# Returning expert results to their tokens' rows inside the routed loop instead of gathering them at the end

## The chip, the cores and the metric

The kernel runs on one core of a Trainium2 chip. The metric is the device time of one execution in microseconds (us), the median of several runs. The profile is one execution, whose span runs from its first to its last instruction.

## The reference

A cross-attention block is followed by a mixture-of-experts feed-forward part. Only the second part is touched in substance. There are 4 x 1024 = 4096 tokens of 256 channels, all in fp32:

```
x = x + cross_attention(context, layernorm(x), mask)
f = layernorm(x)                                      # "tokens"
shared = gelu(f @ Wfc_s + bfc_s) @ Wproj_s + bproj_s  # 256 -> 1024 -> 256
p = softmax(f @ Wr); the two largest of 8, divided by their sum, are the gates
routed = sum over the two chosen experts e of gate_e * (gelu(f @ Wfc[e] + bfc[e]) @ Wproj[e] + bproj[e])
out = x + shared + routed
```

## The kernel before

It is six blocks, one after another: `prepare` (layer norms, weights cut into high and low parts), `attention` (about two thirds of the time; it also clears the DRAM tensor `routed` with one DMA of the ACT queue), `project_out` (writes `tokens`), `route` (computes `slots`, the row in `routed` of each of the 2 x 4096 token-expert pairs), `experts` and `combine`.

**experts.** Rows are worked on in tiles of 256: m = 0 to 15 are the shared expert's (SHARED = 16), m = 16 to 55 the routed experts' (ROUTED = 40). In step m, TensorE (PE) alternates between the first layer of tile m+1 (`fc`, four parts) and the second layer of tile m (`proj`, four parts), and after `proj` part 2 transposes the input of tile m+2. That is 100 matrix instructions a step. ACT does the gelu and the high half of the second weights (`upper_w2`), DVE cuts the hidden values (`hidden`), cuts the transposed input (`lower_x`) and adds the bias into `y[:, s]` (s is m's parity), and POOL makes the low half of the second weights (`lower_w2`, line 1342, twice a step). Each matrix product is three matmuls of high and low parts.

The SP queue issues, in a fixed order per routed step m: the load of the input `xt` of tile m+2 (`load_x`), four quarter loads of the first weights of tile m+3, two half loads of the second weights of tile m+2, the small first bias, then, behind a wait for `y` of tile m (`s_yv`), the store of `y` to `ys` (line 1315) and the load of the second bias. So the next step's `load_x` is queued behind that wait.

During the shared tiles POOL fills `routed`: for each of 32 tiles of 128 tokens it loads the tile into one of four buffers `moved` (line 1355) and, three tiles later, writes each row of it to its two places in `routed` with two indirect DMAs (line 1361). Before it loads into a buffer again it waits for both scatters from it. SP's first `load_x` from `routed` (step 14, for tile 16) waits until all 64 scatters have landed (line 1289).

**combine.** For 16 pairs of 128-token tiles POOL gathers rows of `ys` with four indirect DMAs a pair (line 1545), into four buffers `c_y`. DVE multiplies them by the gates and adds them to `x2` (line 1559, four instructions a pair), and SP stores the pair to the output (line 1566).

Of the kernel before, what the change touches and what calls it, by code (L numbers as in the profile page):

```python
# [5 lines left out]
F32 = mybir.dt.float32  # L6
# [29 lines left out]
ROUTED += ROUTED % 2  # L36
ROWS = (ROUTED + 1) * TS


# [314 lines left out]
def attention(nc, qn_g, kn_g, lnT, wHead, maskRow, maskCol, attT, routed, Wfc_s, Wfc, w1S):  # L354
# [6 lines left out]
    with ExitStack() as ctx:  # L361
# [28 lines left out]
        o_sb = t.sb("o_sb", [DH + 1, 2, 512])  # L390
        zero = t.sb("zero", [P, D])
        gain2 = t.sb("gain2", [P, DH])
        most2 = t.sb("most2", [P, 1])
# [32 lines left out]
        def _(sp):  # L426
# [56 lines left out]
            either(sp, attend)  # L483
            sp.wait_ge(s_clear, 16)
            for q in range(QB):
# [6 lines left out]
        def _(pool):  # L492
# [156 lines left out]
        def _(act):  # L649
            def window(w):  # L650
                for u in range(UNITS):
# [11 lines left out]
                    for name, m in w.jobs(u):  # L663
# [12 lines left out]
                        else:  # L676
# [4 lines left out]

            act.wait_ge(s_zero, 1)
# [483 lines left out]
def experts(nc, weights_s, weights, w1S, expert, slots, tokens, routed, x2, ys):  # L1166
# [3 lines left out]
    with ExitStack() as ctx:  # L1170
        t = Tools(nc, ctx)
        ident = t.sb("f_ident", [P, P])
        moved = t.sb("moved", [P, 4, D])
        xt = t.sb("xt", [P, 2, 2, D])
        xT_hi = t.sb("xT_hi", [P, 2, C, TS], F32R)
# [17 lines left out]
        s_xt, s_xh, s_xlo, s_h, s_y, s_yv = (t.sem("f_" + n) for n in ("xt", "xh", "xlo", "h", "y", "yv"))  # L1193
        s_g, s_hh, s_hl = ([t.sem("f_%s_%d" % (n, i)) for i in range(4)] for n in ("g", "hh", "hl"))
        s_mv, s_sc = ([t.sem("f_%s_%d" % (n, i)) for i in range(4)] for n in ("mv", "sc"))
# [3 lines left out]
        ys_v = ys.rearrange("(t r p) d -> t p r d", r=2, p=P)  # L1199
        S2, LAST = SHARED // 2, (SHARED + ROUTED) // 2 - 1  # L1200
# [31 lines left out]
        def _(sp):  # L1232
# [30 lines left out]
            def load_x(src, tile, parity):  # L1263
                sp.dma_start(xt[:, parity:parity + 1], src[bass.ds(tile, 1)].rearrange("t p r d -> p t r d")).then_inc(s_xl[parity], 16)

# [63 lines left out]
            sp_pair(LAST - 1, False, 4)  # L1329
            sp_pair(LAST, False, 2)  # L1330
            for s in range(2):
                sp.wait_ge(s_ys[s], 16 * ROUTED // 2)

        @block.gpsimd
        def _(pool):
# [27 lines left out]

            def pair(U, last=False):
                for s in range(1 if last else 2):
                    for h in range(2):
                        lower_w2(1 - s, h, U * 2 + (s + 3 - SHARED))

            with pool.Fori(S2, LAST) as u:
                pair(u)  # L1370
            pair(LAST, True)

# [111 lines left out]
        def _(dve):  # L1484
# [18 lines left out]
            def step(U, s, shared, left):  # L1503
                m = U * 2 + s
                slot, n = next_slot(U, s, shared, 0)
                for p in range(4):
                    if left >= 1:
                        hidden(m + 1, p, 1 - s)
                    if p == 2 and left >= 2:
                        lower_x(m + 2, s)  # L1510
                dve.wait_ge(s_b2[slot], n * 16)
                dve.wait_ge(s_y, m * 4 + 4)
                if not shared and not (isinstance(U, int) and U == S2):
                    dve.wait_ge(s_ys[s], (U - S2) * 16)
                v.tensor_tensor(y[:, s], ps_y[:, s, :, 0:D], b2[:, slot].unsqueeze(1).broadcast_to([P, 2, D]),
# [8 lines left out]

def combine(nc, x2, slots, gates, ys, out):

    NB, PAIRS = 4, TT // 2
    with ExitStack() as ctx:  # L1528
# [7 lines left out]
        @block.gpsimd  # L1536
        def _(pool):
            for k in range(PAIRS):
                i = k % NB
                if k >= NB:  # L1540
                    pool.wait_ge(s_y[i], 64 * (k // NB))
                    pool.wait_ge(s_sum, 2 * (k - NB + 1))  # L1542
                for tile in range(2):
                    for j in range(2):
                        pool.indirect_dma_start(out=y[:, i, tile, j, :], out_offset=None, in_=ys[:, :],  # L1545
                                                in_offset=bass.IndirectOffsetOnAxis(ap=slots[:, j, 2 * k + tile:2 * k + tile + 1], axis=0)
                                                ).then_inc(s_y[i], 16)

        @block.vector
        def _(dve):  # L1550
            for k in range(PAIRS):
                i = k % NB
                dve.wait_ge(s_y[i], 64 * (k // NB + 1))
                for j, done in enumerate((s_half, s_sum)):
# [6 lines left out]

        @block.sync
        def _(sp):
            for k in range(PAIRS):
                sp.wait_ge(s_sum, 2 * k + 2)
                sp.dma_start(out_v[k], x2[:, 2 * k:2 * k + 2, :]).then_inc(s_out, 16)
            sp.wait_ge(s_out, 16 * PAIRS)

# [6 lines left out]
def cross_attention_moe(nc, x, ctx_in, mask, ln_x_g, ln_x_b, ln_l_g, ln_l_b, qn_g, kn_g, Wq, Wkv, Wout, bout,  # L1575
# [10 lines left out]
    tokens = dram("tokens", TOKENS, D)  # L1586
    routed = dram("routed", ROWS, D)
    ys = dram("ys", ROUTED * TS, D)
    w1S = dram("w1S", 2 * (E + 1), P, 4, 2, 2, P)
    prepare(nc, x, ctx_in, mask, ln_x_g, ln_x_b, ln_l_g, ln_l_b, Wq, Wkv, lnT, wHead, maskRow, maskCol)  # L1590
    attention(nc, qn_g, kn_g, lnT, wHead, maskRow, maskCol, attT, routed, Wfc_s, Wfc, w1S)
    with ExitStack() as ctx:
# [8 lines left out]
        experts(nc, [bfc_s, Wproj_s, bproj_s], [bfc, Wproj, bproj], w1S, expert, slots, tokens, routed, x2, ys)  # L1601
        combine(nc, x2, slots, gates, ys, out)

# [18 lines left out]
```

## Time and profile before

| | |
|---|---|
| median of 3 runs | 3173.11 us (3171.98 to 3178.89) |
| profiled execution, its own time | 3178.12 us |
| its span | 3176.6 us |
| busy over the span | PE 89%, ACT 64%, DVE 61%, POOL 47% |
| DMA | 345.19 MB, 109 GB/s in the mean |

A busy share over the whole span is a mean over stages with different limits, so it doesn't say what bounds a stage. "DMA share" is the mean busy share of the core's 16 DMA engines; q1 is the SP queue's ring, q0 POOL's, q10 ACT's. PEclk is TensorE's granted clock as a share of full speed (1.00 is 2.4 GHz, 0.50 is 1.2 GHz).

### The profile page before, as it was taken

The page shows a single profiled execution, that of the slowest core. Times are in us where ns is not written, and L with a number is a line of the kernel's source. Part 1 is how long each engine was busy: PE and PEld are TensorE (multiplying, and loading weights), DVE is VectorE, ACT ScalarE, POOL GpSimd, SP SyncE. Part 2 cuts the span into 40 slices and gives each one's busy share as a digit, 9 for nine tenths or more (in the row PEclk, how much of TensorE's full clock was granted, in tenths as well). Part 3 has the DMA queues.
Part 4 walks back from the last instruction along what each step waited for, and adds up shares of the span by engine and source line. Part 5 has one row for each costly group of instructions (what it writes and reads, how often), then busy time and mean ns, then how long its engine had stood idle before and what let it go on. Part 6 is the DMA issues. An engine that isn't in the chain of part 4 may idle for free. (4 is left out here: it accounts for less than half of the span.)

```text
span 3176.6 us, 55807 instructions
## 1 busy us (share of the span) xinstructions
PE 2830.3 (89%) x18170; PEld 2529.0 (80%) x18170; DVE 1942.5 (61%) x2783; ACT 2041.2 (64%) x4217; POOL 1479.1 (47%) x875
## 2 busy tenths in 40 slices
PE   2599999999999999999999999964766999999980
PEld 1588888888888888888888888854766999999980
DVE  6366666667666666666666776644555555555543
ACT  2388888888888888888888888851112334445430
POOL 1355454455455454554544554542433533443447
PEclk7799999999999999999999999986777999999995
DMA  7611010110110210110210100129964249999965
GB/s 265 228 41 37 25 43 32 60 43 32 31 38 23 69 42 25 38 36 25 73 32 29 45 32 30 38 66 185 212 138 140 98 137 316 320 321 321 320 213 148
DMA packets 227050, 345.19 MB, mean 109 GB/s; under 512 B 45657, under 2 KB 132398, under 8 KB 223419
## 3 DMA queue, kind: packets, MB, share of 16 engines
q1 hardware_dynamic: 201882, 279.87, 30.0%
q0 software_dynamic: 14608, 54.02, 5.1%
q10 hardware_dynamic: 10512, 10.75, 1.0%
q8 instruction: 21, 0.34, 0.0%
q14 instruction: 27, 0.21, 0.0%
HBM read 254.65 MB, written 89.92 MB: 108 GB/s over the span
## 5 line engine op out<-in xcount | busy, mean ns | idle before, releaser
L623 DVE TENSOR_TENSOR pr_lo<-pr,pr_hi 128x512 fp32r<-128x512 f32 x1152 | 1111.6, 971 | 615.1 <-ACT pr_hi L662 601.7
L661 ACT ACTIVATE pr<-ps_s 128x512 f32<-128x512 f32 x1024 | 613.6, 599 | 273.9 <-PE ps_s L774 260.3
L662 ACT ACTIVATE pr_hi<-ps_s 128x512 fp32r<-128x512 f32 x1024 | 607.5, 593 | 0.0
L695 PEld LDWEIGHTS ps_m<-w_sb,lnT_sb 128*128 128x128 f32 x3564 | 491.4, 193 | 76.4 <-issue 25.3
L708 PE MATMUL ps_o<-pr_hi,vA 128*128 128x512 f32 x1152 | 509.2, 442 | 7.9 <-DVE pr_lo L623 7.9
L695 PE MATMUL ps_m<-w_sb,lnT_sb 128*128 128x192 f32 x3564 | 482.6, 272 | 25.2 <-issue 25.0
L772 PE MATMUL ps_s<-qT,kT 128*128 128x512 f32 x1152 | 465.8, 404 | 0.8 <-ACT qT L679 0.8
L774 PE MATMUL ps_s<-qT,kT 65*128 65x512 f32 x1152 | 456.0, 396 | 0.0
L709 PE MATMUL ps_o<-pr_hi,vC 128*128 128x512 f32 x1152 | 453.0, 393 | 0.0
L710 PE MATMUL ps_o<-pr_lo,vA 128*128 128x512 f32 x1152 | 451.8, 392 | 0.0
L1457 ACT ACTIVATE ht<-f_ps_h,b 128x256 f32<-128x256 f32 x448 | 188.2, 471 | 341.6 <-PE f_ps_h L1396 317.0
L517 POOL TENSOR_TENSOR rs<-ss,minus_half 128x18 f32<-128x18 f32 x66 | 238.8, 3617 | 285.2 <-DVE ss L640 285.2
L1396 PE MATMUL f_ps_h<-xT_hi,w 128*128 128x256 f32 x1792 | 364.5, 286 | 1.5 <-ACT ht L1457 1.5
L1342 POOL TENSOR_TENSOR w<-w2raw,w 128x1024 fp32r<-128x1024 f32 x82 | 198.5, 2422 | 321.9 <-ACT w L1443 321.9
L1409 PE MATMUL f_ps_y<-w,h_hi 128*128 128x256 f32 x1792 | 326.9, 281 | 0.3 <-issue 0.3
L1396 PEld LDWEIGHTS f_ps_h<-xT_hi,w 128*128 128x128 f32 x1792 | 296.9, 193 | 1.8 <-issue 1.8
L1493 DVE CAST h_hi<-ht 128x512 fp32r<-128x512 f32 x224 | 115.3, 515 | 275.3 <-ACT ht L1457 261.3
L1409 PEld LDWEIGHTS f_ps_y<-w,h_hi 128*128 128x128 f32 x1792 | 275.0, 190 | 0.0
L710 PEld LDWEIGHTS ps_o<-pr_lo,vA 128*128 128x128 f32 x1152 | 216.8, 188 | 51.0
L506 POOL TENSOR_TENSOR k_st<-nrm,k_st 128x576 fp32r<-128x576 f32 x65 | 92.1, 1417 | 354.3 <-DVE q_st L628 354.3
L1396 PE MATMUL f_ps_h<-xT_lo,w 128*128 128x256 f32 x896 | 254.5, 284 | 0.0
L772 PEld LDWEIGHTS ps_s<-qT,kT 128*128 128x128 f32 x1152 | 216.6, 188 | 45.0 <-ACT qT L679 1.0
(181 smaller groups left out, 5103.5 us busy)
## 6 DMA issues: line engine op xcount, KB each, us to landing
w<-w1S_dram SPq DMA_DIRECT2D x164, 512.0 KB, 6.1
w2raw<-in_L_ffn_Wproj SPq DMA_DIRECT2D x80, 512.0 KB, 6.9
w_sb<-wHead_dram SPq DMA_DIRECT2D x68, 384.0 KB, 3.0
w1S_dram<-cut POOLq DMA_DIRECT2D x18, 1024.0 KB, 4.3
attT_dram<-o_sb SPq DMA_DIRECT2D x128, 130.0 KB
a<-attT_dram SPq DMA_DIRECT2D x32, 512.0 KB, 11.9
rb<-rden_dram SPq DMA_DIRECT2D x32, 512.0 KB, 14.7
routed_dram<-zero ACTq DMA_DIRECT2D x1, 10496.0 KB, 43.0
```

Of the source, the lines that this page charges most:

```text
L517: g.tensor_tensor(rs[:, :], ss[:, :], minus_half[:, :], ALU.pow).then_inc(s_pool, 1)
L623: v.tensor_tensor(pr_lo[:, u % RING, :], pr[:, u % RING, :], pr_hi[:, u % RING, :].bitcast(F32), ALU.subtract).then_inc(s_prlo, 1)
L661: act.activation(pr[:, u % RING, :], ps_s[:, u % RING, :], ACT.Exp, bias=bias)
L662: act.activation(pr_hi[:, u % RING, :], ps_s[:, u % RING, :], ACT.Exp, bias=bias).then_inc(s_exp, 1)
L695: ins = mm(out[:, 0:3 * DH], lnT_sb[:, a, c, tile * P:(tile + 1) * P], w_sb[:, w.slot, b, c, :], start=k == 0, stop=k == 3 * C - 1)
L708: mm(ps_o[:, q, :], vA[:, slot, k, :], pr_hi[:, r, :], start=k == 0, stop=False)
L709: mm(ps_o[:, q, :], vC[:, slot, k, :], pr_hi[:, r, :], start=False, stop=False)
L710: mm(ps_o[:, q, :], vA[:, slot, k, :], pr_lo[:, r, :], start=False, stop=last).then_inc(s_pv, 1)
L772: mm(ps_s[:, u % RING, :], kT1[:, w.slot, k * P:(k + 1) * P], qT1[:, w.slot, q * 512:(q + 1) * 512], start=True, stop=False)
L774: mm(ps_s[:, u % RING, :], kT2[0:DH + 1, w.slot, k * P:(k + 1) * P], qT2[0:DH + 1, w.slot, q * 512:(q + 1) * 512], start=False, stop=True) ...
L1396: ins = mm(ps_h[:, p % 2, i, :], w1[:, slot, p, k, lo, i, :], x_[:, parity, k, :], start=k_ == 0, stop=k_ == 3 * C - 1)
L1409: ins = mm(ps_y[:, parity, r, 0:D], h[:, parity, c, r * P:(r + 1) * P], w2[:, slot, p, lo, c % 2, :], start=c == 0 and k_ == 0, stop=c == ...
```

## The change

Each row of `routed` gets a 257th column with the row's "home": 2 x token + k for the k-th choice of a token, which is a row number in a larger `ys` (2 x 4096 rows in token order, and spare rows behind them for the padding of the tiles). While `routed` is cleared, a second DMA writes spare numbers into that column. POOL writes the home numbers into `moved` with an `iota` a tile, and the tile is now loaded twice side by side, so that each of the two scatters carries its own number. `load_x` brings the numbers in with the rows; DVE copies them to `home`, and POOL scatters `y` by them with two indirect DMAs of 128 rows a tile, between its two `lower_w2`. The SP store of `ys` goes. In `combine` a pair is one plain SP DMA of 512 KB, and the output stores move to the ACT queue.

```diff
 # attention: pool, then act
+            pool.iota(spare[:, :], pattern=[[P, ROWS // P]], base=2 * TOKENS, channel_multiplier=1).then_inc(s_zero, 1)
...
-            act.dma_start(routed.rearrange("(t p) d -> p t d", p=P),
+            act.wait_ge(s_zero, 2)
+            act.dma_start(routed[:, 0:D].rearrange("(t p) d -> p t d", p=P),
                           zero[:, :].unsqueeze(1).broadcast_to([P, ROWS // P, D])).then_inc(s_clear, 16)
+            act.dma_start(routed[:, D:D + 1].rearrange("(t p) d -> p t d", p=P),
+                          spare[:, :].bitcast(F32).unsqueeze(2), allow_slow_non_contiguous=True).then_inc(s_clear, 16)
 # experts, sync
             def load_x(src, tile, parity):
-                sp.dma_start(xt[:, parity:parity + 1], src[bass.ds(tile, 1)]...
+                n = src.shape[-1]
+                sp.dma_start(xt[:, parity:parity + 1, :, 0:n], src[bass.ds(tile, 1)]...
...
                     sp.wait_ge(s_xt, m + 1)
+                    if not shared:
+                        sp.sem_inc(s_go, 1)
+                        sp.wait_ge(s_home, m - (SHARED - 1))
...
-                if not shared or later2:
+                if later2:
                     sp.wait_ge(s_yv, m + 1)
-                if not shared:
-                    sp.dma_start(ys_v[bass.ds(m - SHARED, 1)].rearrange("t p r d -> p t r d"), y[:, s:s + 1]).then_inc(s_ys[s], 16)
 # experts, gpsimd: filling routed
-                    pool.dma_start(moved[:, i, :], moved_v[tile]).then_inc(s_mv[i], 16)
+                    pool.iota(moved[:, i, :, D:D + 1].bitcast(I32), pattern=[[1, 2], [0, 1]], base=2 * P * tile,
+                              channel_multiplier=2).then_inc(s_num, 1)
+                    pool.dma_start(moved[:, i, :, 0:D], moved_v[tile].unsqueeze(1).broadcast_to([P, 2, D])).then_inc(s_mv[i], 16)
...
+                    pool.wait_ge(s_num, back + 1)
                     for k in range(2):
                         pool.indirect_dma_start(out=routed[:, :], ...,
-                                                in_=moved[:, i, :], in_offset=None).then_inc(s_sc[i], 16)
+                                                in_=moved[:, i, k, :], in_offset=None).then_inc(s_sc[i], 16)
 # experts, gpsimd: the routed tiles
+            def scatter(U, s):
+                pool.wait_ge(s_yv, U * 2 + (s + 1))
+                pool.wait_ge(s_home, U * 2 + (s + 1 - SHARED))
+                pool.sem_inc(s_go, 1)
+                for r in range(2):
+                    pool.indirect_dma_start(out=ys[:, :], out_offset=bass.IndirectOffsetOnAxis(ap=home[:, s, r:r + 1], axis=0),
+                                            in_=y[:, s, r, :], in_offset=None).then_inc(s_ys[s], 16)
+
+            def pair(U, first=False, last=False):
+                for s in range(2):
                     for h in range(2):
-                        lower_w2(1 - s, h, U * 2 + (s + 3 - SHARED))
+                        if not (last and s == 1):
+                            lower_w2(1 - s, h, U * 2 + (s + 3 - SHARED))
+                        if h == 0 and not (first and s == 0):
+                            scatter(U - (1 - s), 1 - s)
 # experts, vector, end of a step
+                if (not shared or isinstance(U, int) and m == SHARED - 1) and left >= 1:
+                    if not shared and not (isinstance(U, int) and U == S2 and s == 0):
+                        dve.wait_ge(s_ys[1 - s], (U - (S2 - s)) * 32)
+                    v.tensor_copy(home[:, 1 - s, :], xt[:, 1 - s, :, D].bitcast(I32)).then_inc(s_home, 1)
                 dve.wait_ge(s_b2[slot], n * 16)
                 dve.wait_ge(s_y, m * 4 + 4)
 # combine
+        ys_v = ys[0:2 * TOKENS, :].rearrange("(g t p j) d -> g p t j d", t=2, p=P, j=2)
+        @block.sync
+                if k >= NB:
+                    sp.wait_ge(s_sum, 2 * (k - NB + 1))
+                sp.dma_start(y[:, i], ys_v[k]).then_inc(s_y[i], 16)
```

## Rows read from the trace of the kernel before

**Rows 1.** Stages: window, its us; busy us (instructions) PE PEld DVE ACT POOL; PEclk, DMA, GB/s.
```profile
2412.00:2611.00 199.00, 195.80 (x1624) 195.06 (x1624) 107.51 (x179) 71.03 (x155) 95.62 (x100) 0.98 0.38 123
2611.00:3084.00 473.00, 472.03 (x3975) 470.57 (x3973) 247.22 (x397) 229.51 (x431) 188.86 (x78) 1.00 0.95 307
3084.00:3176.60 92.60, 0.00 (x0) 0.00 (x0) 28.51 (x65) 0.00 (x0) 63.08 (x64) 0.52 0.47 139
```
**Rows 2.** The chain that ended last, first and last pieces: start us, us, what.
```profile
3086.98 0.63 issue
...
3172.25 0.89 DVE x L1559 x2
```
**Rows 3.** Groups by line: busy us, mean ns of one, idle before and its releasers.
```profile
L1545 POOL DMA_INDIRECT c_y<-ys_dram,slots x64 | 63.1, 986 | 29.0 <-issue 17.4 <-PEq L1528 9.8 <-DVE x L1559 1.8
L1559 DVE SCALAR_TENSOR_TENSOR x<-c_y,gates,x 128x256 f32<-128x256 f32 x64 | 28.3, 483 | 61.5 <-DMA c_y<-ys_dram,slots 61.0
```
**Rows 4.** DMA queues in 3087 to 3174: queue, packets, MB, share of 16 engines.
```profile
q1 hardware_dynamic: 4080, 3.93, 13.1%
```
**Rows 5.** Narrow windows: TensorE restarting after an idle stretch, and after its last work.
```profile
2414.00:2416.00 2.00, 2.00 (x11) 2.00 (x11) 0.69 (x1) 0.91 (x2) 0.00 (x0) 0.50 1.10 351
...
2418.00:2420.00 2.00, 1.06 (x6) 0.79 (x4) 0.00 (x0) 1.97 (x4) 2.00 (x2) 0.77 1.05 388
...
3088.00:3090.00 2.00, 0.00 (x0) 0.00 (x0) 0.00 (x0) 0.00 (x0) 1.60 (x2) 0.50 0.23 66
```
**Rows 6.** Timeline of POOL, filling `routed`: start, us, instruction, [idle before and its releaser].
```profile
2468.79 0.58 POOL L1355 DMA_DIRECT2D moved<-tokens_dram  x1 [1.73 <-DMA routed_dram<-moved,slots]
...
2473.65 0.58 POOL L1355 DMA_DIRECT2D moved<-tokens_dram  x1 [1.71 <-DMA routed_dram<-moved,slots]
```
**Rows 7.** Timeline of SP's queue: first input load from `routed`.
```profile
2587.90 0.38 SPq L1264 DMA_DIRECT2D xt<-routed_dram  x1
```
**Rows 8.** Timeline of PE: transposes of tile 16, the first routed one.
```profile
2599.27 0.60 PE L1381 MATMUL f_ps_t<-f_ident,xt 128*128 128x128 f32 x4
```
**Rows 9.** Timeline of POOL in `route`: the kernel's iotas.
```profile
2375.91 0.57 POOL L1081 IOTA eight<- 128x256 f32 x1
2376.43 0.71 POOL L1083 IOTA tiles<- 128x336 f32 x1
```
**Rows 10.** One line, L914 (POOL's 256 KB store of `tokens`): duration and landing.
```profile
L914 POOL DMA_DIRECT2D tokens_dram<-l x16: 733/746/751, 2187.0 to 2371.0; - x16
...
DMA to landing us min/median/max: 2.6/9.2/11.1
```
**Rows 11.** One line, L1315 (SP's 256 KB store of `ys`): landing.
```profile
DMA to landing us min/median/max: 2.1/5.5/6.3
```
**Rows 12.** DMA queues in 2630 to 3060 (routed tiles).
```profile
q1 hardware_dynamic: 103488, 137.62, 98.9%
```
**Rows 13.** DMA queues in 2290 to 2340 (`project_out`).
```profile
q1 hardware_dynamic: 9639, 9.54, 101.7%
```
**Rows 14.** Timeline of all engines around one routed step.
```profile
2670.42 0.60 PE L1381 MATMUL f_ps_t<-f_ident,xt 128*128 128x128 f32 x4
...
2674.43 0.68 DVE L1515 TENSOR_TENSOR y<-f_ps_y,b 128x512 f32<-128x512 f32 x1
...
2676.41 0.37 SPq L1264 DMA_DIRECT2D xt<-routed_dram  x1
...
2677.21 2.42 POOL L1342 TENSOR_TENSOR w<-w2raw,w 128x1024 fp32r<-128x1024 f32 x1 [3.71 <-ACT w L1443]
```
**Rows 15.** Timeline of DVE: bias adds of the next step and of the last tile.
```profile
2686.28 0.69 DVE L1515 TENSOR_TENSOR y<-f_ps_y,b 128x512 f32<-128x512 f32 x1
...
3083.53 0.69 DVE L1515 TENSOR_TENSOR y<-f_ps_y,b 128x512 f32<-128x512 f32 x1 [4.08 <-issue]
```
**Rows 16.** One line, L1381 (input transposes): idle until, us, times.
```profile
  DMA xt<-routed_dram: 1.6, 6
```
**Rows 17.** DMA issues of the whole trace: the clearing of `routed`, KB, us to landing.
```profile
routed_dram<-zero ACTq DMA_DIRECT2D x1, 10496.0 KB, 43.0
```

More of the change, by code:

```diff
@@ L37 @@
 ROWS = (ROUTED + 1) * TS
+WIDE = D + 1
 class Tools:
@@ L391, in attention @@
         zero = t.sb("zero", [P, D])
+        spare = t.sb("spare", [P, ROWS // P], I32)
         gain2 = t.sb("gain2", [P, DH])
@@ L483, in _ @@
             either(sp, attend)
-            sp.wait_ge(s_clear, 16)
+            sp.wait_ge(s_clear, 32)
             for q in range(QB):
@@ L1172, in experts @@
         ident = t.sb("f_ident", [P, P])
-        moved = t.sb("moved", [P, 4, D])
-        xt = t.sb("xt", [P, 2, 2, D])
+        moved = t.sb("moved", [P, 4, 2, WIDE])
+        home = t.sb("home", [P, 2, 2], I32)
+        xt = t.sb("xt", [P, 2, 2, WIDE])
         xT_hi = t.sb("xT_hi", [P, 2, C, TS], F32R)
@@ L1194, in experts @@
         s_g, s_hh, s_hl = ([t.sem("f_%s_%d" % (n, i)) for i in range(4)] for n in ("g", "hh", "hl"))
+        s_home, s_num, s_go = t.sem("f_home"), t.sem("f_num"), t.sem("f_go")
         s_mv, s_sc = ([t.sem("f_%s_%d" % (n, i)) for i in range(4)] for n in ("mv", "sc"))
@@ L1198, in experts @@
         routed_v = routed.rearrange("(t r p) d -> t p r d", r=2, p=P)
-        ys_v = ys.rearrange("(t r p) d -> t p r d", r=2, p=P)
         S2, LAST = SHARED // 2, (SHARED + ROUTED) // 2 - 1
@@ L1263, in load_x @@
             def load_x(src, tile, parity):
-                sp.dma_start(xt[:, parity:parity + 1], src[bass.ds(tile, 1)].rearrange("t p r d -> p t r d")).then_inc(s_xl[parity], 16)
+                n = src.shape[-1]
+                sp.dma_start(xt[:, parity:parity + 1, :, 0:n], src[bass.ds(tile, 1)].rearrange("t p r d -> p t r d")).then_inc(s_xl[parity], 16)
             load_x(tokens_v, 0, 0)
@@ L1329, in _ @@
             sp_pair(LAST - 1, False, 4)
-            sp_pair(LAST, False, 2)
+            sp_pair(LAST, False, 1)
             for s in range(2):
-                sp.wait_ge(s_ys[s], 16 * ROUTED // 2)
+                sp.wait_ge(s_ys[s], 32 * ROUTED // 2)
         @block.gpsimd
@@ L1359, in _ @@
                     pool.wait_ge(s_mv[i], 16 * (back // 4 + 1))
+                    pool.wait_ge(s_num, back + 1)
                     for k in range(2):
                         pool.indirect_dma_start(out=routed[:, :], out_offset=bass.IndirectOffsetOnAxis(ap=slots[:, k, back:back + 1], axis=0),
-                                                in_=moved[:, i, :], in_offset=None).then_inc(s_sc[i], 16)
-            def pair(U, last=False):
-                for s in range(1 if last else 2):
-                    for h in range(2):
-                        lower_w2(1 - s, h, U * 2 + (s + 3 - SHARED))
-            with pool.Fori(S2, LAST) as u:
+                                                in_=moved[:, i, k, :], in_offset=None).then_inc(s_sc[i], 16)
[8 more added lines that the diff above has]
+                for s in range(2):
+                    for h in range(2):
+                        if not (last and s == 1):
+                            lower_w2(1 - s, h, U * 2 + (s + 3 - SHARED))
+                        if h == 0 and not (first and s == 0):
+                            scatter(U - (1 - s), 1 - s)
+            pair(S2, first=True)
+            with pool.Fori(S2 + 1, LAST) as u:
                 pair(u)
-            pair(LAST, True)
+            pair(LAST, last=True)
+            scatter(LAST, 1)
         @block.tensor
@@ L1513, in step @@
                 if not shared and not (isinstance(U, int) and U == S2):
-                    dve.wait_ge(s_ys[s], (U - S2) * 16)
+                    dve.wait_ge(s_ys[s], (U - S2) * 32)
                 v.tensor_tensor(y[:, s], ps_y[:, s, :, 0:D], b2[:, slot].unsqueeze(1).broadcast_to([P, 2, D]),
@@ L1522, in _, with combine @@
             loops(dve, step, first=1)
-def combine(nc, x2, slots, gates, ys, out):
-    NB, PAIRS = 4, TT // 2
+def combine(nc, x2, gates, ys, out):
+    NB, PAIRS_ = 4, TT // 2
     with ExitStack() as ctx:
@@ L1534, in combine, with _ @@
         out_v = out.rearrange("b (g t p) d -> (b g) p t d", t=2, p=P)
-        @block.gpsimd
-        def _(pool):
-            for k in range(PAIRS):
+        ys_v = ys[0:2 * TOKENS, :].rearrange("(g t p j) d -> g p t j d", t=2, p=P, j=2)
+        @block.sync
+        def _(sp):
+            for k in range(PAIRS_):
                 i = k % NB
                 if k >= NB:
[L1541 to L1547, printed above, removed]
+                    sp.wait_ge(s_sum, 2 * (k - NB + 1))
+                sp.dma_start(y[:, i], ys_v[k]).then_inc(s_y[i], 16)
         @block.vector
         def _(dve):
-            for k in range(PAIRS):
+            for k in range(PAIRS_):
                 i = k % NB
-                dve.wait_ge(s_y[i], 64 * (k // NB + 1))
+                dve.wait_ge(s_y[i], 16 * (k // NB + 1))
                 for j, done in enumerate((s_half, s_sum)):
@@ L1560, in _ @@
                                                        ALU.mult, ALU.add).then_inc(done, 1)
[L1562 to L1567, printed above, removed]
+        @block.scalar
+        def _(act):
+            for k in range(PAIRS_):
+                act.wait_ge(s_sum, 2 * k + 2)
+                act.dma_start(out_v[k], x2[:, 2 * k:2 * k + 2, :]).then_inc(s_out, 16)
+            act.wait_ge(s_out, 16 * PAIRS_)
 NAMES = ["x", "ctx_1024", "mask_BxS2_bf1"] + ["L0_xattn_" + n for n in (
@@ L1586, in cross_attention_moe @@
     tokens = dram("tokens", TOKENS, D)
-    routed = dram("routed", ROWS, D)
-    ys = dram("ys", ROUTED * TS, D)
+    routed = dram("routed", ROWS, WIDE)
+    ys = dram("ys", 2 * TOKENS + ROWS, D)
     w1S = dram("w1S", 2 * (E + 1), P, 4, 2, 2, P)
@@ L1601, in cross_attention_moe @@
         experts(nc, [bfc_s, Wproj_s, bproj_s], [bfc, Wproj, bproj], w1S, expert, slots, tokens, routed, x2, ys)
-        combine(nc, x2, slots, gates, ys, out)
+        combine(nc, x2, gates, ys, out)
 def kernel(**inputs):
```

1 line of the change is left out of this document (removed).

## Prediction

> **What bounds the kernel now.** I read the stages first, as windows [rows 1], because a share over the span hides them. From 2412 to 3084 TensorE is the bound: it is busy 195.8 of 199.0 us in the shared tiles and 472.0 of 473.0 us in the routed ones, at 2.4 GHz. In the routed stage the DMA share is 0.95 as well, so there are two limits close together. After 3084 TensorE does nothing for 92.6 us. The chain that ended last lies wholly in that tail, from 3086.98 to the last DVE pair at 3172.25 [rows 2]. The groups by line say what sets its pace: POOL's 64 indirect DMAs are busy 63.1 us and sit idle 29.0, of which 17.4 is the 0.30 us dispatch gap between them, while DVE works 28.3 us and waits 61.5 for gathered rows [rows 3]. So `combine` is bound by POOL making descriptors, and is the place to gain. The rest of the reading asks what the change costs in the two TensorE-bound stages.
>
> **Term 1, combine.** It runs from 3086.9 to 3176.6, 89.7 us. After the change POOL is out of it. DVE has 28.3 us of work, with waits between halves and pairs some 31. The DMA engines move 8.39 MB in (16 loads of 512 KB in 2 KB pieces) and 4.19 MB out. With 2 KB weight pieces they moved 388 GB/s [rows 5]: 8.39 MB take 21.6 us. The output stores took 13.1% of 87 us, 11.4 us [rows 4]. Together 33 us, just above DVE. Around it: 0.4 us to start, 3 for the first load, 2.5 for the last store and its landing, which is 39, and I take 40. Bounds: 37 (DVE alone), 51 (reads and writes together at half that rate beyond DVE's pace, as in the mixed stages). Saving 50 (39 to 53).
>
> **Term 2, the last tile.** Its `y` ends at 3084.2 [rows 15]. The store then landed in about 2.1 us [rows 11]. Two indirect DMAs of 0.99 with gaps of 0.30 [rows 3] end 2.6 us later, and a scatter's landing took 1.73 after its last instruction [rows 6]: 4.3, so +2.2 us.
>
> **Term 3, filling `routed`.** One iteration takes 4.9 us, of which POOL waits 1.73 for the scatter it has just issued [rows 6]. So whatever is added to an iteration adds to the loop. The iota: 256 elements 0.57, 336 elements 0.71 [rows 9], so 0.12 plus 1.75 ns an element, and for two elements with its gap 0.2. The load with twice the descriptors: the store of 256 rows took 0.75 against 0.58 [rows 6, 10], +0.17. One more wait 0.05. Rows of 1028 bytes at odd addresses in the scatter: not in this trace, nothing at the low end, and at the high end twice the descriptors in two instructions (0.34) and a wait longer by half (0.9); I take 0.1, as all rows of 1 KB and more here behave alike. Sum 0.52 (0.4 to 1.9), and 28 iterations that wait and 4 that don't make 16 us (12 to 55). What covers it: the first load from `routed` is issued at 2587.9 [rows 7] and transposed at 2599.27 [rows 8]; 2.6 us of landing leave 8.7 us. Beyond that TensorE stands still, and with it all that follows. So +7.5 us (3 to 46). TensorE's clock suffers too. After its last work, whose bias add is at 3083.53, it is at 1.2 GHz in 3088 to 3090; and when it restarted near 2413 it stayed there until about 2419, with 11 matmuls in 2 us [rows 5] where a full rate is 17 (3975 in 473 us [rows 1]). That is 6.2 us at two thirds of the rate: +2 (0 if the clock holds through the stall).
>
> **Term 4, the routed steps.** A step is 11.85 us (2674.43 to 2686.28 [rows 14, 15]). POOL gets two indirect DMAs, 2.6 us beside 4.8 of `lower_w2`, and fits. DVE gets a copy of two elements, some 0.15 us in a stage where it is half idle [rows 1]. SP loses the `ys` store and gains a wait that is long met. What matters is the new wait of DVE: before it may copy the homes of tile m+1 it needs the scatter of tile m-1 to have landed, and behind that copy stand `y` of tile m, SP's next input load and the transposes that need it. Count from the start S of a step's matmuls, 2673.6, three quarters of a microsecond before `y` in the trace. `lower_w2` runs from S+3.6 to S+6.0 [rows 14], the two indirect DMAs start at S+6.35 and S+7.65. The copy is wanted at S+12.5. The input load has almost no slack today: it is issued at S+2.8, used 5.9 us later (2670.42 plus 11.85 is 2682.3), and TensorE waited for it 6 times, 1.6 us in all [rows 14, 16]. But the removed store frees 0.4 us and some register work of SP, and 0.8 us of the same ring ahead of it (256 KB at 307 GB/s [rows 1]). So the copy may come up to 1.2 us late, S+13.6, and the second scatter has 5.95 us from its start. Unloaded, it takes 1.0 + 1.73 = 2.7 [rows 6]. Loaded: in `project_out`, with SP's ring as full (101.7% [rows 13]), POOL's 256 KB store landed in 9.2 us against 2.6 at least [rows 10]. In the routed stage SP's own 256 KB stores add 3.4 to their least (5.5 against 2.1 [rows 11]), about half of the excess there. I take 2.7 plus half of 3.4, 4.4 to 5 us: no stall, with about 1 us in hand. Bounds: 2.7, and 9.3.
>
> Here a rule of the Trainium skill can be weighed. The trace shows a store of four data packets an engine waiting 6.6 us beyond its least in a full stage [rows 10]. The page "DMA: Bandwidth & Descriptors" (Queues, rings and completion order) says that an engine goes round the queue rows at packet granularity, so that POOL's ring would wait for one packet of SP's at each of its own. By that rule the scatter would land in about 3 us and this term has no risk at all; the trace doesn't agree, and the sum goes by the trace.
>
> DMA work itself: the routed stage is at 98.9% with 66 ns a packet [rows 12] (430 us x 16 x 0.989 / 103488). Bytes stay equal but for 1 KB a tile. The 256 input pieces of a tile grow to 1028 bytes; if each costs 0 to 100% more, that is 0 to 1.05 us a step (256 / 16 x 66 ns) against 0.13 of free share. I take 10%, which fits, and 3 us over 40 steps for what doesn't (0 to 37).
>
> **At nothing:** POOL's `spare` iota delays what follows it at the start by 0.3 us, which I count. The 4-byte column, 10496 pieces, follows the clearing, which landed in 43 us [rows 17], and lies beside the long attention block, where TensorE works from data loaded ahead; without that cover it would be 10496 / 16 x 66 ns, 43 us.
>
> **Sum:** -50 + 2.2 + 7.5 + 2 + 3 + 0.3 = -35 us. The profiled span 3176.6 (3178.1 with what lies around it) becomes 3142 (3143); the median, 5 us below that execution, becomes 3138.
>
> **Rivals.**
> *A, the landing wait rules the routed steps (slower).* Each microsecond by which the second scatter lands later than 5.95 us after its start costs 39 us. For: the 9.2 us of rows 10, and small POOL transfers have no priority there. Against: SP's ring is emptier here, and a stall empties it further. The gain is gone at 6.9 us. At 9.3 us less the relief, say 8.5: +100, 3238 us.
> *B, filling `routed` takes 1.3 us more an iteration (odd addresses, dearer iota).* 42 - 8.7 = 33 instead of 7.5, so 3164. For: nothing in the trace has such rows. Against: the iota rows.
> *C, the DMA engines become the bound of the routed stage.* A third more for each input piece: 0.35 - 0.13 = 0.22 us a step, +9; at 100% more, +37. 3144 to 3172.
> *D, combine doesn't get faster than 60 us* because reads and writes hinder each other: 3158. Against: 388 GB/s in rows 5.
>
> **How the numbers follow.** No change can be told within 0.2%, 6.3 us. Main case 0.52, own range 3122 to 3152. B 0.12, C 0.12, D 0.06, faster nearly all (C at its high end the same). A 0.18, of which 0.03 mild and near the old time, 0.15 slower. Faster 0.80, same 0.05, slower 0.15. The range 3120 to 3177 leaves out A's slow part and a little at the low end.
>
> **What would show it.** Combine near 40 us with DVE busy over 70% of it; the last scatter landing near 3088 plus the shift; POOL's iteration 5.4 us, the load of line 1264 from `routed` near 2604, TensorE idle 5 to 10 us before the transposes of tile 16 and a dip in the clock; then steps of 11.85 us. Wrong if steps are 12.5 us or more (A or C; in A the idle time of PE is before the transposes and DVE waits for a scatter, in C the share is full and loads land late), or if the idle stretch is 20 us or more (B).

## The result, and the profile after

The changed kernel takes 3182.03 us (median of 12 runs, 3177.32 to 3189.87), the kernel before 3173.70 us in 12 runs beside them (3168.54 to 3179.48). The ratio is 1.0025 (1.0016 to 1.0035): a quarter of a per cent slower, just above what this measurement can tell from no change. Forecast were 3138 us and a gain. The profiled execution took 3180.82 us, with a span of 3179.3.

A gain of 50 us was made, and lost again in four other places. I cut both spans at the same events of the program: y0 is the start of the first bias add of `experts`, y15 that of the last shared tile, y55 that of the last tile.

| stretch, us | before | after | difference | forecast |
|---|---|---|---|---|
| start of the span to y0 | 2436.1 | 2460.7 | +24.6 | +0.3 |
| y0 to y15: shared tiles, filling `routed` | 179.0 | 181.3 | +2.3 | +9.5 |
| y15 to y55: 40 routed steps | 468.4 | 486.3 | +17.9 | +3 |
| y55 to the first read of `ys` in `combine` | 4.1 | 12.2 | +8.1 | +2.2 |
| from there to the end | 89.0 | 38.8 | -50.2 | -50 |
| span | 3176.6 | 3179.3 | +2.7 | -35 |

**The stages.** The windows of [rows 1], read from the changed kernel's trace: window, its us, busy us (instructions) of PE, PEld, DVE, ACT, POOL, then PEclk, DMA share and GB/s. The fourth row is a stretch of routed steps alone.
```profile
2412.00:2611.00 199.00, 174.93 (x1437) 173.51 (x1437) 107.90 (x197) 63.68 (x138) 95.24 (x127) 0.92 0.41 134
2611.00:3084.00 473.00, 456.60 (x3816) 451.90 (x3815) 299.42 (x421) 221.97 (x416) 261.87 (x149) 1.00 0.91 298
3084.00:3179.00 95.00, 42.48 (x356) 41.87 (x354) 52.46 (x101) 17.86 (x34) 26.42 (x17) 0.76 0.68 231
2660.00:3080.00 420.00, 407.12 (x3402) 402.82 (x3402) 269.93 (x373) 201.62 (x374) 242.24 (x136) 1.00 0.94 307
```
The first row has 21 us of TensorE work less than before because all of it comes later. In the second TensorE is no longer busy throughout: 456.6 of 473 where it was 472.0. The last row shows that this loss is spread over the routed steps, with the DMA engines less busy than before. The kernel before, in a stretch of routed steps alone:
```profile
2630.00:3060.00 430.00, 429.78 (x3621) 428.73 (x3620) 225.05 (x361) 211.92 (x398) 176.49 (x73) 1.00 0.99 320
```
Its share was 0.99 at 320 GB/s, and is now 0.94 at 307. So it isn't bandwidth.

**The start.** ACT's timeline around the two DMAs: start, us, instruction, idle before it.
```profile
90.23 0.46 ACTq L686 DMA_DIRECT2D routed_dram<-zero  x1
90.71 43.52 ACTq L688 DMA_DIRECT2D routed_dram<-spare  x1
135.50 0.78 ACT L675 ACTIVATE raw<-ps_m 128x192 f32<-128x192 f32 x3 [53.95 <-issue]
```
The clearing is issued in 0.46 us. The second DMA, 4 bytes for each of 10496 rows, holds ACT's queue for 43.52 us in its issue, and the first `raw` of `attention` waits behind it. The hold isn't a wait for the clearing to land: it ends at 134.2, and the clearing lands at 143.8, 53.6 us after its issue. PE's timeline has the consequence:
```profile
105.61 4.13 PE L700 MATMUL ps_m<-w_sb,lnT_sb 128*128 128x192 f32 x18 [25.48 <-issue]
135.88 12.05 PE L700 MATMUL ps_m<-w_sb,lnT_sb 128*128 128x192 f32 x90 [26.14 <-ACT raw L675]
```
After 18 matmuls TensorE has to wait until ACT empties `ps_m`, and stands still for 26.14 us. In the kernel before these are one piece of 108 matmuls from 104.79 on.

**The routed steps.** The waits of all engines in 2380 to 3180: engine, line, what it waited for, us in total, times, longest.
```profile
DVE home L1539 <- DMA ys_dram<-y,home: 74.9, 34, 3.6
...
ACT w L1468 <- DMA w2raw<-in_L_ffn_Wproj: 37.9, 35, 2.5
...
PEld f_ps_t L1406 <- DMA xt<-routed_dram: 21.1, 21, 3.6
```
DVE waits 34 times for a scatter to land before it may overwrite `home`, TensorE 21 times for the input load queued behind (one of these is at tile 16, 3.6 us; the other 20 come to 17.5 us). [Rows 16] had 6 times and 1.6 us. One such step, near the end, is in DVE's timeline:
```profile
3101.50 0.17 DVE L1539 COPY home<-xt 128x2 int32<-128x2 int32 x1 [2.76 <-DMA ys_dram<-y,home]
3101.77 0.69 DVE L1544 TENSOR_TENSOR y<-f_ps_y,b 128x512 f32<-128x512 f32 x1
```
and what SP had queued behind that bias add (SP's timeline):
```profile
3102.63 0.35 SPq L1264 DMA_DIRECT2D b<-in_L_ffn_bproj  x1
3103.10 0.38 SPq L1271 DMA_DIRECT2D xt<-routed_dram  x1
```
The copy starts 2.76 us late, the bias add with it, and the next step's input is asked for only then. Scatter to landing can be read as the start of a waiting copy minus the start of that scatter's second indirect DMA: a median of 6.9 us over 34 tiles (5.8 to 8.1).

**The filling.** POOL's timeline, to be set beside [rows 6]:
```profile
2596.91 0.13 POOL L1363 IOTA moved<- 128x2 int32 x1 [1.63 <-DMA routed_dram<-moved,slots]
2597.00 0.76 POOL L1365 DMA_DIRECT2D moved<-tokens_dram  x1
```
An iteration takes 5.37 us in the mean of the last 27, where it took 5.11. The first load from `routed` comes at 2623.27, 35.4 us later than [rows 7]; 24.6 of these are the start's. PE's timeline at the first routed tile has the stall:
```profile
2626.03 0.66 PE L1406 MATMUL f_ps_t<-f_ident,xt 128*128 128x128 f32 x4 [3.42 <-DMA xt<-routed_dram]
```

**The end.** The last indirect DMA and the first load of `combine` (timelines of POOL and SP), and the waits of SP's queue in 3110 to 3200:
```profile
3131.08 0.96 POOL L1381 DMA_INDIRECT ys_dram<-y,home  x1 [0.30 <-issue]
...
3140.53 2.13 SPq L1572 DMA_DIRECT2D c_y<-ys_dram  x4
```
```profile
SPq L1340 <- DMA ys_dram<-y,home: 20.1, 1, 20.1
...
SPq L1175 <- PEq L1175: 6.7, 1, 6.7
```
SP's load comes at 3140.53, and 6.7 us before that, at 3133.8, it has the last landing behind it, at most 1.8 us after the last indirect DMA was executed (3132.04). It stands those 6.7 us at the barrier that ends the block `experts`. It is the move to `combine` that is late, not the data. What holds the barrier is in POOL's queue: an instruction DRAIN at the block's end (line 1175, in the kernel before line 1170), here after and before (duration in ns, start):
```profile
L1175 POOLq DRAIN  x1: 10222/10222/10222, 3130.1 to 3130.1; - x1
```
```profile
L1170 POOLq DRAIN  x1: 10375/10375/10375, 3075.4 to 3075.4; - x1
```
Now it ends at 3140.3, 8.2 us after POOL's last indirect DMA, and everyone goes on 0.2 us later. Before, it ended at 3085.8, 7.9 us after POOL's last `lower_w2` (3077.84), and nobody noticed, since SP came to the barrier only at 3086.6 and waited 0.2 us.

The chain that ended last, first and last pieces, answers to [rows 2], and the group of DVE to [rows 3]:
```profile
3141.27 5.88 DMA c_y<-ys_dram
...
3174.93 0.89 DVE x L1584 x2
```
```profile
L1584 DVE SCALAR_TENSOR_TENSOR x<-c_y,gates,x 128x256 f32<-128x256 f32 x64 | 27.9, 482 | 19.9 <-DMA c_y<-ys_dram 19.3
```
DVE now works 27.9 us and waits 19.9, where it waited 61.5.

### The profile page after: what moved, and what is told of

It reads as the page before. It is cut to its first block and busy times, and to the rows that moved or that the text cites. A ratio compares the mean times of both kernels' runs of the same rounds, so it can differ in the third digit from the quotient of the medians.

```text
span 3179.3 us, 56020 instructions
## 1 busy us (share of the span) xinstructions
PE 2835.1 (89%) x18170; PEld 2530.7 (80%) x18170; DVE 2007.5 (63%) x2823; ACT 2042.9 (64%) x4217; POOL 1514.3 (48%) x924
## 5 line engine op out<-in xcount | busy, mean ns | idle before, releaser
L1434 PE MATMUL f_ps_y<-w,h_lo 128*128 128x256 f32 x896 | 252.0, 281 | 0.0
## 6 DMA issues: line engine op xcount, KB each, us to landing
routed_dram<-zero ACTq DMA_DIRECT2D x1, 10496.0 KB, 53.6
```

Source lines behind the costliest of these rows:

```text
L1434: ins = mm(ps_y[:, parity, r, 0:D], h[:, parity, c, r * P:(r + 1) * P], w2[:, slot, p, lo, c % 2, :], start=c == 0 and k_ == 0, stop=c == ...
```

## The experiments

All edits are to the changed kernel. "A step" is the mean over the 40 from y15 to y55: 11.71 us before, 12.16 after. The last of them is short, so a full step of the kernel before is the 11.85 of the prediction. Where one execution is given, the table's stretches decide, not the time.

**late: the column's DMA later.** The same DMA is issued at the start of ACT's second attention window, when the clearing has landed.
```diff
+                if isinstance(w.v, int) and w.v == 0 and w.s == 1:
+                    act.dma_start(routed[:, D:D + 1]..., spare...).then_inc(s_clear, 16)
...
-            act.dma_start(routed[:, D:D + 1]..., spare...).then_inc(s_clear, 16)
```


> The column of spare numbers is written by the same ACT DMA, but issued one attention window later, before the second head's window, when the clearing of the rows has drained. Theory: in the changed kernel the issue of this DMA held ACT's queue for 43.52 us because the ring was still full of the 10496 pieces of the clearing, and TensorE waited 26 us for ACT's first copies. Then the issue here takes well under 2 us, the first tokens of the routed stage come 24 to 26 us earlier and the kernel takes about 3157 us (25 less than the changed kernel). Rival 1: 10496 pieces of 4 bytes are slow to generate whatever is in the ring: the issue is again some 40 us long, ACT stands still in the middle of attention, and nothing or little is gained. Rival 2: the 4-byte writes slow the loads of weights: the start stays late although ACT is not held.

Measured: 3155.95 us against 3176.94 for the kernel before, ratio 0.9936 (0.9913 to 0.9960). ACT's timeline:
```profile
166.87 0.38 ACTq L655 DMA_DIRECT2D routed_dram<-spare  x1
```
The issue takes 0.38 us and not 43.52, y0 is at 2432.2, and the other stretches stay (steps 490.0, end 12.2). So the hold comes with the clearing in front of it and not with the DMA's shape alone, and it had turned the kernel from faster to slower.

**homecopy: POOL takes its own copy of the homes.** DVE then no longer waits for a landing, only for POOL to have copied; POOL waits for the landing of two tiles earlier, after its first `lower_w2`.
```diff
+                if not (isinstance(U, int) and U == S2):
+                    pool.wait_ge(s_ys[s], (U - S2) * 32)
+                nc.gpsimd.tensor_copy(aim[:, s, :], home[:, s, :]).then_inc(s_aim, 1)
...
-                        dve.wait_ge(s_ys[1 - s], (U - (S2 - s)) * 32)
+                        dve.wait_ge(s_aim, U * 2 + (s - SHARED))
```


> POOL copies the home numbers of a tile from home to a second tile right before it scatters, and DVE's copy of the next homes waits for that copy instead of the scatter's landing. Everything else is as in the changed kernel. Theory: the 40 routed steps went from 11.71 to 12.16 us because DVE waited 74.9 us in 34 steps for a scatter to land, which made y, then SP's next input load, then the transposes late (37.6 us of waits for inputs). Then DVE waits for nothing there, steps come back to 11.85 us, and the kernel is 15 to 18 us faster than the changed one, about 3165 us. Rival: input pieces of 1028 bytes and the scatters make the DMA engines the bound; then the DVE wait goes but steps stay above 12.1 us and the kernel gains under 5 us.

Measured: 3166.46 us against 3176.94, ratio 0.9962 (0.9950 to 0.9973). The routed steps take 466.7 us, 11.67 each. The window of its routed steps:
```profile
2670.00:3080.00 410.00, 410.00 (x3463) 410.00 (x3462) 228.54 (x380) 202.80 (x382) 253.36 (x175) 1.00 0.98 321
```
TensorE is busy throughout, with the same scatters running and the DMA share even higher. So the loss in the steps was the wait alone; neither the added traffic nor its form costs the steps anything. Its filling stretch was 187.0 us, 5.7 longer than in the changed kernel. PE's timeline and a window behind it show where these went, in the one execution that was profiled, the slowest of nine:
```profile
2635.79 1.12 PE L1413 MATMUL f_ps_t<-f_ident,xt 128*128 128x128 f32 x4 [6.67 <-DMA xt<-routed_dram]
```
```profile
2636.00:2640.00 4.00, 4.00 (x20) 4.00 (x20) 0.69 (x1) 1.10 (x3) 0.00 (x0) 0.50 0.94 268
```
TensorE stood 6.67 us before tile 16, where it was 3.42, and then ran at a granted clock of 0.50 (1.2 GHz). Why POOL's filling was slower there (5.57 us an iteration) stays open; with the same copy in `allfix` it was 5.40.

**plainstore: no scatters.** SP stores `y` in tile order as before; the last part reads the same number of rows, in the wrong order. What is left out is the scatters and DVE's wait. The rows of 1028 bytes, the iotas and the copies stay.
```diff
+                    sp.dma_start(ys_v[bass.ds(m - SHARED, 1)]..., y[:, s:s + 1]).then_inc(s_ys[s], 16)
...
-                        if h == 0 and not (first and s == 0):
-                            scatter(U - (1 - s), 1 - s)
...
-                        dve.wait_ge(s_ys[1 - s], (U - (S2 - s)) * 32)
```


> Leaves out the scatters of y: SP stores y plainly as in the kernel before (so the last part reads rows in the wrong order), DVE copies the homes without a wait, inputs are still rows of 1028 bytes. If the scatter and its wait are the whole cost of the routed steps, they come back to 11.71 to 11.85 us and the transposes hardly wait. If the 1028-byte rows cost DMA time, the steps stay longer, 11.95 or more, and the input waits stay. The gap between last bias add and the last part's first load, 12.2 us in the changed kernel, goes back to about 3.5 us.

Measured: 3152.01 us in one execution. Steps 467.9 us in all (468.4 before), end of the block 3.3 us, start still 2462.3. Of the waits in 2380 to 3180 one of interest is left, and SP's queue passes the barrier at once:
```profile
PEld f_ps_t L1406 <- DMA xt<-routed_dram: 1.6, 4, 0.5
```
```profile
SPq L1175 <- PEq L1175: 0.2, 1, 0.2
```
Input pieces of 1028 bytes cost nothing, which is the end of rival C. SP isn't held at the barrier, and POOL's last work, a `lower_w2`, ended 8.8 us before SP got there (3104.17 against 3113.0). So even a DRAIN that ended 8.2 us later would have been hidden; here it took 4.2 us, and why it was shorter than the 10.4 of the kernel before isn't shown.

**halfloads: a quarter less traffic.** The scatters and DVE's wait stay, but each load of first weights in the routed loop fetches only half its bytes, in as many pieces, of 1 KB where they were 2 KB (the other half stays stale). It asks whether the landing is long because of SP's ring.
```diff
-                        load1(1 - s, p, e1)
+                        load1(1 - s, p, e1, 256)
```


> Leaves out half of each first-weight load of the routed tiles inside the loop (the other half of the weights is stale), so SP's ring carries 1 MB less of 3.8 MB a step; all else as in the changed kernel. In the changed kernel a scatter lands 6.9 us after the start of its second indirect DMA (median of 34), against 2.7 us while routed is filled. Theory: it waits behind what SP's ring has outstanding at that moment, so with a quarter less traffic it lands in 3 to 5 us, DVE's waits for it (74.9 us in 34 steps) fall under 20 us, and the steps come to 11.7 to 11.9 us. Rival: the landing is slow by itself here (scattered rows of y, receipts of the writes) and stays at 6 us or more, with steps above 12.0.

Measured: 3164.54 us in one execution. The window of routed steps, and its waits:
```profile
2660.00:3060.00 400.00, 400.00 (x3380) 400.00 (x3379) 232.64 (x371) 198.11 (x373) 236.50 (x136) 1.00 0.77 231
```
```profile
DVE home L1539 <- DMA ys_dram<-y,home: 30.3, 33, 1.9
...
PEld f_ps_t L1406 <- DMA xt<-routed_dram: 2.6, 1, 2.6
```
The share falls from 0.94 to 0.77, the landing from 6.9 to 5.96 us, and the steps are back at 11.66. DVE still waits, 0.9 us each time, and nobody behind it in the steps is late (the one wait of 2.6 us is at tile 16). That agrees with the forecast's threshold of 5.95 us but doesn't measure it, since input loads have a less busy ring here too. And the landing fell by 1 us only, not to the 3 to 5 that I expected. The number of pieces in SP's ring stayed, and whether the landing goes by their number wasn't tried. 2.7 us is what the forecast worked out for an unloaded pair; where the other 3.3 are spent at a share of 0.77 stays open.

**tailwait: POOL waits for its last scatters itself,** before it leaves the block. The theory was that leaving is slow because DMAs are under way.
```diff
             scatter(LAST, 1)
+            for s in range(2):
+                pool.wait_ge(s_ys[s], 32 * ROUTED // 2)
```


> As the changed kernel, but POOL itself waits at its end for all scatters to have landed. In the changed kernel the data of the last scatter moved by 3133 and SP's wait for it ended there, yet the last part began at 3140.5. Theory: POOL reaches the barrier at the end of the block only some 8 us after its last indirect DMA, because it has to drain a DMA that is in flight; if an explicit wait for the landing replaces that, the gap from the last bias add to the first load falls from 12.2 to about 6 us. Rival: the 8 us are a fixed cost of leaving the block after indirect DMAs: the gap stays 12 us.

Measured: 3195.71 us in one execution. From y55 to `combine` 13.9 us, not less. SP's wait at the barrier:
```profile
SPq L1175 <- PEq L1175: 8.4, 1, 8.4
```
The DRAIN of POOL's queue starts only when POOL has seen its scatters land:
```profile
L1175 POOLq DRAIN  x1: 8228/8228/8228, 3147.9 to 3147.9; - x1
```
The theory falls: with nothing of POOL's under way the DRAIN takes 8.2 us all the same. The wait is added to the time to leave, it doesn't take its place.

**merged: no barrier.** The loads, sums and stores of the last part stand in the block of `experts`, behind SP's wait for the scatters.
```diff
+            for k in range(PAIRS_):
+                i = k % NB
+                if k >= NB:
+                    sp.wait_ge(s_sum, 2 * (k - NB + 1))
+                sp.dma_start(c_y[:, i], pairs_v[k]).then_inc(s_cy[i], 16)
...
-        combine(nc, x2, gates, ys, out)
```


> As the changed kernel, but the last part's loads, sums and stores stand in the block of the experts: SP goes on to them when the last scatters have landed, with no barrier of all engines in between. A wait of POOL for its own scatters had not shortened the gap (13.9 against 12.2 us). Theory: POOL needs some 8.4 us to leave a block after its last indirect DMA, wait or no wait, and only the barrier makes the others see it. Then the gap from the last bias add to the first load falls from 12.2 to about 5.5 us, and the kernel gains about 6 us. Rival: the time lies in what SP does itself after such a wait; then the gap stays.

Measured: 3176.31 us in one execution; 5.25 us from y55 to the first read, where 12.2 were. The last part takes 37.1. The landing of the last scatter can now be read: executed at 3136.18, the read at 3137.70 (timelines of POOL and SP).
```profile
3135.22 0.96 POOL L1392 DMA_INDIRECT ys_dram<-y,home  x1 [0.30 <-issue]
...
3137.70 6.02 SPq L1351 DMA_DIRECT2D c_y<-ys_dram  x5
```
So the data cost about 1 us more than before (5.25 against 4.1) and the way out of the block 7. POOL's DRAIN is still there, 10.2 us long, but no engine needs to wait for it before the last part.

**lag2: a tile is scattered two iterations after its load, not three,** so that the wait for a buffer's old scatters has one iteration more.
```diff
-                if tile >= 3:
-                    back = tile - 3
+                if tile >= 2:
+                    back = tile - 2
```


> As the changed kernel, but while routed is filled, a tile is scattered two tiles after its load was issued instead of three. The wait before a buffer is loaded again is then for the scatter issued two iterations ago, not the one just issued. Theory: an iteration of 5.37 us is 3.7 us of POOL's own work and 1.7 us of waiting for that landing, so it falls to 3.7 to 4.0 us, the first load from routed comes over 30 us earlier, and TensorE's stall before the transposes of tile 16, about 3.4 us, goes. Rival: the loads don't land within two iterations and POOL waits for them instead; the iteration stays near 5 us.

Measured: 3184.20 us in one execution. POOL's timeline shows an iteration without a wait, 3.5 us long:
```profile
2476.05 0.78 POOL L1365 DMA_DIRECT2D moved<-tokens_dram  x1
2477.12 1.13 POOL L1372 DMA_INDIRECT routed_dram<-moved,slots  x1 [0.30 <-issue]
2478.55 0.97 POOL L1372 DMA_INDIRECT routed_dram<-moved,slots  x1 [0.30 <-issue]
2479.54 0.42 POOL L1363 IOTA moved<- 128x2 int32 x1
2479.63 0.77 POOL L1365 DMA_DIRECT2D moved<-tokens_dram  x1
```
The first load from `routed` comes 138.8 us after y0 instead of 162.5, 24 us earlier and not the 30 that I expected. The shared tiles take 177.7 us, 3.6 less than in the changed kernel, and the stall at tile 16 is gone. The time isn't better, because this execution came to y0 only at 2468.7. Kernels with the long issue got there anywhere from 2460.7 to 2468.9. Part of this spread is in the start itself: TensorE's last matmul of `pr_hi` and `vA` in `attention` comes at 2139.7 to 2144.3 (2112.9 before, 2112.5 to 2113.9 with the column later). The rest is between there and y0, 318.0 to 327.2 us, mostly in `project_out`, which no edit touches; kernels with the short issue have it too (318.3 to 324.1). Its reason is open.

**allfix: late, homecopy and merged together.** It has no edit of its own.

> The changed kernel with three repairs together: the column of spare numbers issued one window later, the home numbers copied by POOL before each scatter, and the last part in the experts' block. Theory: the gains add up, 25 + 16 to 20 + 6 us: 3132 to 3137 us, ratio 0.985 to 0.988 to the kernel before. If one of them only hid behind another, it is 3145 or more.

Measured: 3126.61 us (3123.05 to 3128.26) against 3173.24, ratio 0.9847 (0.9829 to 0.9864), 5 us better than the low end of what I expected. Stretches: 2437.8, 179.9, 466.7, 5.24, 37.1.

**allfix2: allfix and lag2.**

> The same with the scatter two tiles behind the load while routed is filled. Theory: another 3 to 5 us (TensorE's stall before tile 16): 3128 to 3133 us. Rival: the faster scatters hinder the input loads or weights of the shared tiles and nothing is gained.

Measured: 3120.85 us (3118.10 to 3124.41), ratio 0.9829 (0.9812 to 0.9846), the fastest of all. Stretches: 2436.1, 177.8, 466.7, 5.25, 37.1. Of the gain over `allfix`, 2.2 us are in the shared tiles, where the edit is, and 1.7 in the start, where it isn't. Its stages:
```profile
2412.00:2586.00 174.00, 171.01 (x1424) 170.84 (x1425) 95.41 (x157) 63.01 (x137) 101.23 (x132) 0.98 0.46 144
2586.00:3080.00 494.00, 494.00 (x4173) 494.00 (x4172) 274.23 (x458) 236.89 (x449) 282.88 (x196) 1.00 0.92 300
3080.00:3122.90 42.90, 0.45 (x4) 0.25 (x3) 28.52 (x65) 0.00 (x0) 2.04 (x3) 0.55 0.84 303
```
TensorE is busy without a gap from 2586 to 3080, through tile 16 and all routed steps. What is left of its idle time is the last 43 us.

## Why the prediction was wrong, step by step

**Start: the step that turned the sign.** The forecast put the column of spare numbers "at nothing", since it "lies beside the long attention block", and priced it at 43 us "without that cover". The cover was right for the engines' work and wrong for its issue. I costed when the pieces are moved, and not how long the issuing queue is held while 10496 pieces of the DMA in front are still to go. ACT has work behind that instruction 16 us later, and TensorE lives on what ACT evicts. `late` shows it: 0.38 us for the same issue, and the start back at 2432. The cost at y0 is 25 us in the changed kernel's profile, and 25 to 33 over all with the long issue; read at the end of `attention`, before the spread of `project_out`, it is 27 to 31. It was in no rival. With this step alone right, the forecast would have been about 3163 us.

**Term 4, the routed steps: right mechanism, wrong size of the landing.** The forecast named the wait, the copy, the bias add and the input load behind it, and the threshold of 5.95 us; `homecopy` shows this chain by taking the wait away, and `halfloads`, where scatters land in 5.96 us and no step is late, is in line with the threshold. Mis-sized was the landing: "2.7 plus half of 3.4, 4.4 to 5 us", measured 6.9. I had taken half the excess of SP's own stores, though the nearest row of a POOL transfer beside a full ring of SP's [rows 10] had 9.2. The price above the threshold was too high: 39 us for each us would make 0.95 x 39 = 37, measured are +17.9. Of 74.9 us that DVE waited, TensorE's waits for inputs in the steps show 17.5; that the rest was covered by what the input load had in hand, and that a stall eases the traffic it waits for, is my reading and wasn't tested. Rival A came true in its mild form. It said "the gain is gone at 6.9 us", and the landing was 6.9 and the gain was gone, but that is a coincidence: this term cost half of what A would have it cost, and the start took the other part.

The forecast also weighed a rule of the Trainium skill (page "DMA: Bandwidth & Descriptors", section "Queues, rings and completion order"), made about 3 us of it and found that the trace disagrees. That 3 us took a packet of the page for one piece in the trace, of 66 ns. The page puts typically 9 to 17 descriptors in one packet. If a piece is one descriptor, POOL's four packets an engine wait 4 x 0.6 to 4 x 1.1 us, and with the unloaded 2.7 us the landing would be 5 to 7 us, an estimate from that page's figure. The 6.9 us measured at a share of 0.94 and the 5.96 at 0.77 don't speak against the rule, then, though the 9.2 us of [rows 10] are still more than it gives.

**Term 2, the last tile: half of it was missing.** Forecast +2.2, measured +8.1. The data are there after about 1 us more than before (`merged`). The other 7 us are POOL's way out of the block, which the forecast had put at nothing: its DRAIN ends 8.2 us after its last indirect DMA, and all engines wait for it. The trace of the kernel before had this DRAIN, ending 7.9 us after POOL's last work, but 0.8 us before SP came. What the change did was to move POOL's last work to the end of the block. `tailwait` shows that the DRAIN isn't a wait for unfinished DMAs; what it does in its 8 us stays open.

**Term 3, the filling: right mechanism, sizes too high.** An iteration got 0.26 us longer (forecast 0.52; the 4.9 us there was one iteration, the mean was 5.11). Counted from y0, the first load from `routed` comes 10.8 us later (forecast 16), and the stall at tile 16 was 3.4 us (7.5). The granted clock stayed at 1.00 behind it, so the 2 us for the clock didn't come about here; in `homecopy`, whose stall was 6.67 us, the clock did fall. Rival B falls. That this stall follows POOL's pace is shown by all the traces together: where the first load from `routed` comes 138.8 to 161.1 us after y0 (`lag2`, `allfix2`, `merged`, `plainstore`, `late`), TensorE stands at most 0.4 us before tile 16, and where it comes at 161.3 to 165.8 (`allfix`, changed kernel, `halfloads`, `tailwait`, `homecopy`), 2.0 to 6.7 us. (In `late` and `plainstore` TensorE had also lost over 1 us just before, in short holds whose reason the trace doesn't name.)

**DMA work and rival C.** The 3 us for pieces of 1028 bytes were nothing: `plainstore` has them and its steps are no longer than before, nor are those of `homecopy`.

**Term 1, combine: right.** 38.8 us where 40 were forecast, with DVE busy 27.9 of it; rival D falls. "DVE busy over 70%" holds with 72%.

**The sum.** -35 was forecast, +2.7 measured in the span: +24.3 from the start, +14.9 from the steps, +5.9 from the tail, -7.2 from the filling and the clock, -0.2 from combine. `allfix` takes back what the first three cost, and lands 11 us below the forecast of 3138.

## What to carry to other kernels

A DMA of very many pieces can hold its queue's engine far longer than its usual issue if another such DMA is still under way in front of it in the same queue: put it on an engine with nothing to do, or later, and look at the issue's duration, not only at the landing. A buffer that a scatter on POOL's queue reads is best not waited for by an engine in the middle of the main loop; a private copy of the two home numbers in each partition was enough to take 20 us out of 40 steps. And when work is moved from the end of a kernel to POOL in the loop, look at what POOL does last before a barrier, and at the sequencer's own instructions there: a DRAIN that is hidden before the change can stand in the open behind it.

## What the runs showed of the hardware

- The issue of a 10496-piece DMA on ACT's queue took 43.5 to 46.7 us right behind another one of 10496 pieces, and 0.38 us when that had landed. In the changed kernel the hold ended 9.6 us before the DMA in front had landed. What it waits for in that time the trace doesn't name.
- At the end of the block `experts` a DRAIN of POOL's queue ended 8.2 to 8.3 us after POOL's last indirect DMA in every kernel whose POOL ends the block with a scatter, and took 8.2 us in `tailwait`, where the scatters had landed first. In the kernel before it ended 7.9 us after a `lower_w2`, in `plainstore` 1.7.
- A scatter of 256 rows on POOL's queue landed 6.9 us (median of 34) after the start of its second instruction at a DMA share of 0.94, and 5.96 at 0.77; at the end, with SP's ring empty, in at most 2.7 (3131.08 to 3133.8).
- A DVE cast that takes 0.43 us as a rule took 1.8 to 2.7 us 20 times in the routed stage of the changed kernel, as here (timelines of DVE and POOL). The mean of its group rose from 515 to 656 ns. All 20 began while a `lower_w2` of POOL ran, and ended 0.1 us after the start of the indirect DMA behind it. In the kernel before and in the routed steps of `homecopy` no cast took over 1.5 us. That POOL's work holds them wasn't tested by itself.
```profile
3102.38 0.42 DVE L1518 CAST h_hi<-ht 128x512 fp32r<-128x512 f32 x1
...
3103.70 2.37 DVE L1518 CAST h_hi<-ht 128x512 fp32r<-128x512 f32 x1 [0.18 <-ACT ht L1482]
```
```profile
3103.03 2.76 POOL L1350 TENSOR_TENSOR w<-w2raw,w 128x1024 fp32r<-128x1024 f32 x1 [5.31 <-ACT w L1468]
3105.94 0.99 POOL L1381 DMA_INDIRECT ys_dram<-y,home  x1 [0.16 <-issue]
```
